# Gated delta rule on one Trainium2 core: query length sums in four parts, the last z quarter in two halves

## The reference

```
q = _rmsnorm(q) * inv ; k = _rmsnorm(k) * inv
T = solve_triangular(eye + M, eye)              # per chunk of 64
v_c = T @ v_beta ; k_cumdecay = T @ (k_beta * exp(g))
# one step of the recurrence over the 8 chunks
v_new = v_i - kcd_i @ state
out_i = (q_i * exp(g_i)) @ state + attn @ v_new
state = state * exp(g_last) + (k_i * exp(g_last - g_i)).T @ v_new
# afterwards
h = norm_w * rmsnorm(core) * silu(z) ; out = h @ W_out.T
```

## Time and profile before

| | us |
|---|---|
| median of 3 runs (lowest to highest) | 2488.62 (2487.84 to 2489.73) |
| the profiled execution | 2487.8 |
| its span | 2486.0 |
| PE, matmuls busy | 2375.4 (96%) |
| PE, weight loads busy | 1850.3 (74%) |
| POOL busy | 1729.1 (70%) |
| DVE busy | 1625.5 (65%) |
| ACT busy | 1461.4 (59%) |

### The profile page before, as it was taken

One profiled execution on the slowest core, in us unless ns is written; L12 is line 12 of the kernel. 1 busy time (PEld: TensorE's weight loads), 2 busy tenths in 40 slices (PEclk: granted clock), 3 DMA queues, 4 the chain that ended last, 5 costly groups with the idle time before them and its releaser, 6 DMA issues.

```text
span 2486.0 us, 101436 instructions
## 1 busy us (share of the span) xinstructions
PE 2375.4 (96%) x44496; PEld 1850.3 (74%) x44496; DVE 1625.5 (65%) x2859; ACT 1461.4 (59%) x3270; POOL 1729.1 (70%) x1774
## 2 busy tenths in 40 slices
PE   3899999999999999999999999999999999999898
PEld 2687777777877777778777777778777777786544
DVE  5666676667666676677666766676667666765422
ACT  3766666665666656666666666666666666565211
POOL 2777777778877777788777777787777777887200
PEclk9999999999999999999999999999999999999999
DMA  3211110111111101111111101111111011111100
GB/s 100 54 37 35 43 29 24 35 43 30 38 38 35 43 14 39 35 43 30 33 43 35 26 26 43 35 35 37 35 43 33 20 35 43 31 38 27 50 18 17
DMA packets 71048, 90.13 MB, mean 36 GB/s; under 512 B 16720, under 2 KB 39376, under 8 KB 70480
## 3 DMA queue, kind: packets, MB, share of 16 engines
q1 hardware_dynamic: 70608, 83.63, 12.9%
HBM read 78.53 MB, written 5.08 MB: 34 GB/s over the span
## 4 chain that ended last, share of the span: by engine, by line
PE 87%; DVE 9%; issue 2%; ACT 2%; DMA 1%; SPq 0%; DVEq 0%; POOLq 0%; POOL 0%; ACTq 0%
PE ps_two L432 10%; PE ps_state L412 10%; PE ps_two L412 9%; PE ps_p L643 6%; PE ps_p L584 5%; PE ps_p L466 5%; PE ps_p L461 5%; PE ps_state L609 3%; PE ps_two L632 3%; PE ps_two L424 3%; PE ps_state L643 2%; PE ps_p L480 2%; DVE Vn L1076 2%; PE ps_state L480 2%; PE ps_p L592 2%; DVE St L1095 2%
## 5 line engine op out<-in xcount | busy, mean ns | idle before, releaser
L1196 POOL TENSOR_TENSOR Sd<-St,el 128x512 f32<-128x512 f32 x192 | 201.2, 1048 | 479.9 <-DVEq L1097 479.1
L1235 POOL TENSOR_SCALAR on<-idx_s,lutb 128x134 f32<-128x134 int32 x480 | 355.6, 744 | 27.1
L1076 DVE TENSOR_SCALAR Vn<-ps_p,bR 128x128 f32<-128x128 f32 x512 | 165.5, 349 | 247.9 <-PE ps_p L558 161.5
L960 DVE SCALAR_TENSOR_TENSOR cacc<-ps_two,cw,cacc 128x1022 f32<-128x1022 f32 (+2 forms) x192 | 245.7, 1280 | 44.1 <-ACT cacc L730 39.0
L960 DVE SCALAR_TENSOR_TENSOR cacc<-ps_state,cw,cacc 128x1022 f32<-128x1022 f32 (+2 forms) x192 | 245.7, 1279 | 39.6 <-ACT cacc L730 34.9
L412 PE MATMUL ps_state<-xnT,w_qkv 128*128 128x256 f32 x1024 | 256.1, 394 | 5.9 <-DVEq L965 5.9
L412 PE MATMUL ps_two<-xnT,w_qkv 128*128 128x256 f32 x1024 | 251.4, 389 | 0.0
L432 PE MATMUL ps_two<-xnT,w_z 128*128 128x512 f32 x512 | 250.4, 612 | 0.3 <-DVE sqk L1039 0.3
L1043 DVE STREAM_TRANSPOSE XW<-XW 128x1024 f32<-128x1024 f32 x160 | 199.3, 1245 | 36.1 <-DVE XW L1053 31.5
L845 ACT ACTIVATE Xs<-XW 64x512 f32<-64x512 f32 x320 | 201.2, 629 | 17.9 <-DVE XW L1053 10.2
L412 PEld LDWEIGHTS ps_state<-xnT,w_qkv 128*128 128x128 f32 x1024 | 185.4, 191 | 32.3 <-DVEq L965 6.3
(11 more groups left out here) (171 smaller groups left out, 6021.2 us busy)
## 6 DMA issues: line engine op xcount, KB each, us to landing
qg<-g_scratch SPq DMA_DIRECT2D x64, 512.0 KB, 7.2
g_st<-g_scratch SPq DMA_DIRECT2D x64, 256.0 KB, 5.6
w_qkv<-in_wqkvz SPq DMA_DIRECT2D x16, 512.0 KB, 3.8
w_z<-in_wqkvz SPq DMA_DIRECT2D x16, 256.0 KB, 3.2
w_o<-in_wout SPq DMA_DIRECT2D x16, 256.0 KB, 2.7
idx_s<-in_idx SPq DMA_DIRECT2D x32, 67.0 KB, 1.8
fw_scratch<-looked_up SPq DMA_DIRECT2D x32, 67.0 KB, 1.7
Kg<-in_x SPq DMA_DIRECT2D x2, 1024.0 KB, 5.7
```

The lines of the kernel that those rows point to most:

```text
L960: dve.scalar_tensor_tensor(dst, both[n][:, :, 0:S - t], cw[:, kind, 3 - t:4 - t], dst, ALU.mult, ALU.add).then_inc(s["taps"], 1)
L1076: dve.tensor_scalar(Vn[:, cur, b], bank[:, 0:P], bR[:, R.par, b, c:c + 1], None, ALU.mult).then_inc(done, 1)
L1196: pool.tensor_tensor(Sd[:, :, :, :], St[:, c % 2, :, :, :], el[:, R.par, :, :, c].unsqueeze(3).broadcast_to([P, BB, RATIO, P]), ALU.mult). ...
L1235: m = pool.tensor_scalar(slots[k], idx_s[:, :], float(k), lutb[:, k:k + 1], ALU.is_equal, ALU.mult)
```

## The change

The query length sums, 16 matmuls behind the old parts of step 0, are cut into four parts of 4 matmuls; the parts stand behind the new parts of steps 1, 2, 4 and 6. z quarter 3 leaves the end of `keys_through`: its first matmul stands before the old parts of step 0, its second behind them, where the query length sums stood. z quarter 3 moves from bank 1 to bank 0, and DVE's first `gated` of a round gets a wait for the gate of z quarter 3. No computation is added or left out.

```
+LENGTHS_AT = {1: 0, 2: 1, 4: 2, 6: 3}
...
-    small = spread([("z", i) for i in range(4)] + (N2 if nxt else []), (0, 1))
+    small = spread([("z", i) for i in range(4)], (0, 1, 0, 0)) + (spread(N2, (0, 1)) if nxt else [])
...
-            def lengths(R, i):
-
-                pe.wait_ge(s["sq"], R.at(2, 2, 2))
-                bank, filled = wait_open(pe, R, "n2", i)
-                for b in range(BB):
-                    for c in range(NC):
-                        n, odd = (b * NC + c) // 2, c % 2
-                        m = pe.matmul(bank[odd * C:(odd + 1) * C, n * WIDE:(n + 1) * WIDE],
-                                      sqk[:, i * BB + b, c * C:(c + 1) * C], ones[:, 0:WIDE], start=True, stop=True)
-                m.then_inc(filled, 1)
-
-            def zproj(R, i):
+            def lengths(R, i, part=0, parts=1):
+
+                bank, filled = ps[R.use("n2", i)[0]], full[R.use("n2", i)[0]]
+                if part == 0:
+                    pe.wait_ge(s["sq"], R.at(2, 2, 2))
+                    wait_open(pe, R, "n2", i)
+                per = BB * NC // parts
+                for n in range(part * per, (part + 1) * per):
+                    b, c, odd = n // NC, n % NC, n % 2
+                    m = pe.matmul(bank[odd * C:(odd + 1) * C, n // 2 * WIDE:(n // 2 + 1) * WIDE],
+                                  sqk[:, i * BB + b, c * C:(c + 1) * C], ones[:, 0:WIDE], start=True, stop=True)
+                if part == parts - 1:
+                    m.then_inc(filled, 1)
+
+            def zproj(R, i, parts=(0, 1)):
                 b, a = i // 2, i % 2
-                bank, filled = wait_open(pe, R, "z", i)
-                for k in range(KD):
+                bank, filled = ps[R.use("z", i)[0]], full[R.use("z", i)[0]]
+                if 0 in parts:
+                    wait_open(pe, R, "z", i)
+                for k in parts:
                     m = pe.matmul(bank[:, :], w_z[:, k, a * P:(a + 1) * P], xnT[:, k, cols(R.par, b)],
                                   start=(k == 0), stop=(k == KD - 1))
-                m.then_inc(filled, 1)
+                if 1 in parts:
+                    m.then_inc(filled, 1)
...
-                zproj(R, 3)
...
                 pe.wait_ge(s["a_c"], R.at(2, 0, 2))
+                zproj(R, 3, (0,))
...
-                    if c == 0 and R.nxt:
-                        lengths(R, 0)
                     if c == 0:
+                        zproj(R, 3, (1,))
...
                     if c == 0 and R.nxt:
                         lengths(R, 1)
+                    if c in LENGTHS_AT and R.nxt:
+                        lengths(R, 0, LENGTHS_AT[c], 4)
...
             def gated(R, i):
+                if i == 0:
+                    wait_read(dve, R, "z", 3)
```

## The result

| | before | after |
|---|---|---|
| median of 4 runs, us | 2488.88 (2487.84 to 2489.73) | 2470.94 (2470.42 to 2471.88) |
| profiled span, us | 2486.0 | 2469.4 |
| ratio to before | | 0.9929, 95% interval 0.9913 to 0.9945 |

The change makes the kernel 0.71% faster, 17.9 us; the forecast was 2470.9, 17.7 us under the median shown then. In both columns PE executes the same 44496 matmul records.

The account below looks back on a forecast made before the run. PE work (87% of the chain) plus three short recurrence holes a round bound the kernel. PE's 0.98 us, cut by ACT and POOL to 0.57 a round, times 31 gives 17.7 us: 2470.9 us, 8 in 10 within 2457 to 2482.

Parts of the forecast that it names:

- Step 0 on PE: PE from z quarter 3 to the first key product: 2.57 us instead of 3.55, so 0.98 us sooner.
- ACT's delay: ACT's gate of z quarter 3, and everything behind it in ACT's order, comes 0.65 us later.
- `norm` at the same time as before: POOL's `norm` of the first output bank, behind ACT's squares, starts at 1054.97 against 1055.00 despite PE's 0.98 us.
- State of step 3 0.45 sooner, of step 5 0.44, step 6 0.57: DVE's states: POOL's `Sd` leaves 0.45 and 0.44 us; at step 6 PE returns 0.20 less 0.07, giving 0.57.
- The parts at nothing: Four length-sum parts, about 0.45 us each, lie in waits before L584; the one into step 3 is 0.07 short.
- The drain at a change of tiling mode: PE at each part: a drain of its own would cost up to 0.76 us a round; charged at nothing.
- The whole gain: Rival: ACT or POOL has unseen slack and all 0.98 us a round arrives, 30.4 us, 2458; 12%.
- Less arrives: Rival: z's second half or the old parts start 0.2 us late on PE; 0.37 a round, 2477 us; 13%.
- Slower: Rival: parts stand in front of a ready state, 1.8 us a round against 0.98 saved, 2514 us; 7%.
- no effect: Rival: ACT and POOL meet the gain in full, their delay growing from 0.65 to 1.1 us; 2488 us; 6%.

Follow-up runs that it names:

- the halves alone: Kernel before with z quarter 3 in two halves around step 0's old parts, length sums whole behind the second: 2496.47 us, ratio 1.0034.
- the doubled parts: Changed kernel with each of the four length-sum parts issued twice, 16 records instead of 8 in each place: 2473.13 us, ratio 0.9936.
- the parts alone: Changed kernel with z quarter 3 whole again at the end of `keys_through`, length sums still in four parts: 2469.96 us, ratio 0.9928.
- the later exponentials: Changed kernel with ACT's two exponentials of the next round's queries moved behind the first squares: 2463.53 us, ratio 0.9902.
- the added copy on ACT: Changed kernel with one extra ACT copy of 512 columns between the exponentials and the first squares of each round: 2489.07 us, ratio 0.9998.

## Why the prediction was right

- **Step 0 on PE** was mis-sized. I put a half of z at 0.99 us from the mean distance of four records; it took 1.06 (1039.56 to the old parts, and 769.85 - 768.79 in the halves alone). In the row of a pair the second record starts 1.13 - 0.59 = 0.54 after the first, where the mean of four was 0.46: the first distance is the dear one, the mean had spread it over three, and two halves pay it twice. Another z quarter of the same round, in the kernel before, stands behind work that is itself 128*128:

```profile
1034.73 1.99 PE L412 MATMUL ps_state<-xnT,w_qkv 128*128 128x256 f32 x8
1036.56 1.88 PE L432 MATMUL ps_two<-xnT,w_z 128*128 128x512 f32 x4
```

There four records take 1.88 us, not 1.98, so they stand (1.88 - 0.59)/3 = 0.43 apart on average, with no dear one. Here the 0.1 us comes where z follows 64*64 work, as both halves do. PE saved 0.85 us and not 0.98, a little less than the lowest of the bounds (0.88).
- **ACT's delay** was mis-sized by the same term: the gate is 2.80 us after z's start, not 2.67, 0.78 later than before and not 0.65.
- **`norm` at the same time as before** held, and with it the time. It came 0.03 us later than before, counted from z, where 0.03 sooner was forecast. The errors of PE and ACT did not add up: what sets the state of step 3 is ACT's chain, and PE's missing 0.13 us only made the wait in front of it shorter. ACT's 0.13 was softened because the squares start 0.10 us before the last exponential's end in the profile (1047.72 against 1047.82), which I had not reckoned with, and from `norm` to `Sd` of step 3 it took 1.29 us, 1.34 before. That these sizes cancel, so that the state of step 3 came 11.86 us after z where 11.85 was forecast, is luck; that ACT's order sets it, and not PE's saving, is not.
- **State of step 3 0.45 sooner, of step 5 0.44, step 6 0.57**: measured 0.44, 0.43, 0.57. The return of 0.20 us at step 6 was as described: L591 starts 0.47 after the state (1056.73 to 1057.20), 0.68 in the earlier trace rows, since the output transposes are done in the longer wait.
- **The parts at nothing**: right, shown by the doubled parts. The tight one at step 2 is 0.07 us late (L591 at 1049.10, 0.55 after its state instead of 0.48), and POOL covered it. In the parts alone, where POOL does not, it was still free in the round shown: a later L591 runs without a break (0.69 us instead of 0.77), and the pair of `Vn` behind it comes closer together (0.63 us instead of the 0.68 of the earlier trace rows). I had charged 0.07 there.
- **The drain at a change of tiling mode** (the Trainium skill, TensorEngine Tiling (Array Packing), Key Properties, which stands under Tiling Modes and not under Overview): the trace shows no second one for a part. A part starts 0.20 us after the last 64*64 record (1048.65 to 1048.85), as the length sums did before (0.19 in the earlier trace rows), and runs into L591 without a pause. The parts cost nothing on top, as I had charged. That L584 paid these 0.19 us itself before the change is not shown by the earlier trace rows: there it starts 0.38 us or more after the last 64*64 record, held by its state.
- **The whole gain** as a rival was wrong for the reason given, and the later exponentials show it: with ACT out of the way nearly all of PE's 0.85 us a round arrives, 25.6 us in all against 0.85 x 31 = 26.4.
- **Less arrives** named the step that went wrong, z's halves too dear on PE. It came in part, 0.13 us instead of 0.2, and cost nothing in the end, for the reasons given under `norm`.
- **Slower** and **no effect**: the added copy on ACT shows how near the second was. with 0.52 us more on ACT the change measured 2489.07.

The best kernel of the study is the change with the later exponentials, 2463.5 us. What stays open: what makes the first z record behind 64*64 work dearer than behind 128*128 work; the traces show both cases, but no run varied it.

## What to carry to other kernels

A piece of work moved on the engine that bounds a kernel moves the moment at which its results are complete; follow that moment through each engine that uses it, in that engine's own order, before the saved time is counted. Where part of an expected gain is missing, look for an engine that has become busy without idle time between what was delayed and what everyone waits for, and move there what nobody needs yet: two exponentials moved behind the squares gave 7.4 us and cost nothing, though the same move in the kernel before was worth nothing. And of a change in two parts measure each alone: here one part gave all of the gain and the other, alone, lost 7 us, yet is worth 8 us once the next obstacle is gone.

## What the runs showed of the hardware

- A run of z matmuls (fp32, 128x512, two records each) behind 64*64 work has its second record 0.54 us behind the first; behind 128*128 work four records stand 0.43 apart (1.88 us against 1.98 for the four). z cut in two around 64*64 work cost 0.2 us more in all (3.75 against 3.55 us).
- From the last 64*64 record to the first 128*64 record PE took 0.20 us (1048.65 to 1048.85), and 8 records more behind it took 0.23 us more (0.48 against 0.25 to L591), without a second pause.
- On ACT the next instruction starts some 0.09 to 0.10 us before the end that the profile gives for the one before (842.46 + 0.61 against 842.98): a copy of 0.61 us delays what follows by 0.52, and the run lost 18.1 us, 0.58 in each round.
